# Output sums behind the scores, key scalings in other steps, and a third feed-forward piece of 128 channels in a one-core windowed-attention kernel

## The reference: six layers of windowed attention and feed-forward beside a state-space part

```python
x = L0_attn_x                                  # 16 sequences x 256 tokens x 128
xn = _layernorm(x)
s = state_space_part(xn)                       # about a tenth of the time, at the start
h = xn
for i in range(6):
    h = attn_layer(shift_tokens(h), Wqkv[i], q_scale[i], k_scale[i], Wo[i]) + h
    h = ffn_layer(shift_tokens(h), ln_g[i], ln_b[i], W1[i], b1[i], W2[i], b2[i]) + h
return x + s * silu(h)

def attn_layer(x, Wqkv, qs, ksc, Wo):          # 16 heads of 64, window 32
    q, k, v = split(x @ Wqkv)
    q, k = l2norm(q) * qs, l2norm(k) * ksc
    q = q * cos * scale + rotate_half(q) * sin * scale
    k = k * cos / scale + rotate_half(k) * sin / scale
    attn = softmax(mask(q @ k_window.T * 8.0)) # own and previous window of 32
    return (attn @ v_window) @ Wo

def ffn_layer(x, g, b, W1, b1, W2, b2):        # 341 inner channels
    xn = (x - mean(x)) / sqrt(var(x) + 1e-5) * g + b
    a, gate = split(xn @ W1 + b1)
    return (a * gelu(gate)) @ W2 + b2
```

## Time and profile before

| | us |
|---|---|
| median of 3 runs | 3596.34 |
| the profiled execution | 3596.09 |
| its span | 3594.3 |
| PE busy | 3394.7 (94%) |
| DVE busy | 3151.4 (88%) |
| ACT busy | 2999.4 (83%) |
| POOL busy | 2877.3 (80%) |
| idle of POOL ahead of L1345 | 460.1 |
| idle of POOL ahead of L1359 | 74.0 |
| idle of POOL ahead of L1365 | 64.3 |
| idle of PE ahead of L847 | 59.6 |

### The profile page before, as it was taken

The page is one execution under the profiler, slowest core; times in us unless marked ns, Lnnn a source line. Parts: engine busy times, 40 slices in busy tenths (PEclk is TensorE's granted clock), DMA queues, the critical chain, the costliest instruction groups (busy, mean ns, idle before and its releaser), DMA issues.

```text
span 3594.3 us, 92498 instructions
## 1 busy us (share of the span) xinstructions
PE 3394.7 (94%) x29710; PEld 2110.8 (59%) x29710; DVE 3151.4 (88%) x10872; ACT 2999.4 (83%) x8812; POOL 2877.3 (80%) x2383
## 2 busy tenths in 40 slices
PE   7887999999999999999999999999999999999998
PEld 3444656656666666666656666666666656666665
DVE  7998988988988888988988988988988988988986
ACT  6554888888888888888888888888888888888887
POOL 6887887888887888887888887888887888887883
PEclk9998999999999999999999999999999999999999
DMA  5443322333323333322333322333332333332332
GB/s 164 141 133 124 113 99 102 108 115 108 115 101 101 106 112 106 116 103 99 107 115 107 116 102 99 110 116 103 115 106 96 108 118 105 114 106 99 106 103 92
DMA packets 261726, 396.22 MB, mean 110 GB/s; under 512 B 45566, under 2 KB 86588, under 8 KB 261244
## 3 DMA queue, kind: packets, MB, share of 16 engines
q1 hardware_dynamic: 261244, 390.30, 32.4%
HBM read 157.91 MB, written 6.03 MB: 46 GB/s over the span
## 4 chain that ended last, share of the span: by engine, by line
PE 53%; DVE 17%; POOL 14%; issue 7%; ACT 6%; DMA 2%; SPq 1%; DVEq 0%; POOLq 0%; ACTq 0%
PE bank L886 9%; PE bank L875 7%; PE bank L847 6%; PE bank L360 5%; PE bank L362 5%; PE bank L361 5%; DVE ab L1610 4%; PE bank L914 4%; PE bank L829 4%; POOL rot L1359 4%; POOL pr L1345 4%; PE bank L856 4%; DVE wide L1502 3%; PE bank L857 3%; DVE sm L1655 2%
## 5 line engine op out<-in xcount | busy, mean ns | idle before, releaser
L1184 ACT ACTIVATE pr<-sm,nb,rq 128x128 f32<-128x128 f32 (+1 forms) x3072 | 1518.0, 502 | 10.8 <-DVE nb L1661 10.7
L1345 POOL TENSOR_TENSOR pr<-pr,rden 128x640 f32<-128x640 f32 x768 | 966.2, 1258 | 460.1 <-DVE rden L1635 457.7
L1359 POOL TENSOR_TENSOR rot<-ab,swp 128x512 f32<-128x512 f32 x760 | 978.0, 1287 | 74.0 <-DMA swp<-ab 73.4
L1610 DVE TENSOR_TENSOR ab<-bank,ltab 128x1024 f32<-128x1024 f32 x760 | 925.1, 1217 | 80.6 <-PE bank L362 66.7
L1655 DVE CUSTOM_DVE_ANT_0 sm<-bank,mask 128x128 f32<-128x128 f32 (+1 forms) x3072 | 839.4, 328 | 47.5 <-PE bank L847 42.1
L1184 ACT ACTIVATION_READ_ACCUMULATOR pr<-sm,nb,rq 128x1 f32 x3072 | 599.5, 195 | 0.0
L847 PEld LDWEIGHTS bank<-rot 64*64 64x64 f32 x12288 | 288.1, 132 | 436.0 <-issue 364.7
L1365 POOL TENSOR_TENSOR rot<-rot,rkb 128x512 f32<-128x512 f32 x384 | 492.3, 1289 | 64.3 <-DMA rkb<-k_scratch 64.1
L1642 DVE COPY pt<-bank 128x512 f32<-128x512 f32 x768 | 531.3, 692 | 10.2
L875 PE MATMUL bank<-pt,vtok 128*64 128x160 f32 (+1 forms) x6144 | 461.6, 292 | 29.4 <-ACT vtok L1198 29.4
L1172 ACT ACTIVATE sq<-bank 128x512 f32<-128x512 f32 x768 | 452.6, 589 | 43.2 <-DVE ab L1610 19.9
(11 more groups left out here) (213 smaller groups left out, 5743.7 us busy)
## 6 DMA issues: line engine op xcount, KB each, us to landing
swp<-ab SPq DMA_DIRECT2D x1520, 128.0 KB, 2.0
rkb<-k_scratch SPq DMA_DIRECT2D x768, 128.0 KB, 2.9
rot<-c_scratch SPq DMA_DIRECT2D x64, 256.0 KB, 3.3
sq<-c_scratch SPq DMA_DIRECT2D x64, 256.0 KB, 3.3
xs<-xT SPq DMA_DIRECT2D x95, 128.0 KB, 2.3
xs<-xT SPq DMA_DIRECT2D x95, 127.5 KB, 2.4
raw<-Wqkv SPq DMA_DIRECT2D x48, 128.0 KB, 2.7
wo<-Wo SPq DMA_DIRECT2D x6, 512.0 KB, 4.6
```

Source lines behind the costliest of these rows:

```text
L1184: ins = act.activation(pr[:, s % 4, i, t, 0:P + WINDOW * t], sm[:, s % 2, i, cs], ACT.Exp, bias=nb[:, s, t, i:i + 1], scale=head_scale(rq, ...
L1345: ins = pool.tensor_tensor(pr[:, e % 4, :, :, :], pr[:, e % 4, :, :, :], rden[:, e, :, :].rearrange("p t i -> p i t").unsqueeze(3) .to_bro ...
L1359: pool.tensor_tensor(rot[:, PAIRS * (j % 2) + j // 2, :], ab_of(j, 0, lead), swp_of(j, lead), ALU.add).then_inc(qk_rot, 1)
L1610: dve.tensor_tensor(ab_both(j, lead).rearrange("p i (b t) -> p i b t", b=GB), seqs(qk_bank(j, lead)[:, :]).unsqueeze(1).to_broadcast(shape ...
```

## The change

It has five parts.

1. `outputs` is called directly behind `scores`, ahead of the entries `dn`, `wo`, `rqT`, `cen` and of `down` and `project_out`.
2. `SCALE_STEPS`: pair 1's scaling moves from step 14 of the turn before to step 0, pair 3's from step 2 to step 4.
3. `SPREAD_STEPS`: pair 5's spread moves from step 4 to step 5.
4. `KEYS_FIRST`: at step 13 pair 7's scaling stands ahead of the rotation.
5. `FCH`: the third piece of the feed-forward is channels 213 to 340, 128 wide; its first 43 channels repeat those of the second piece, and their rows of `w2` are zero (one memset).

```diff
-FCH = [(0, 128), (128, 128), (256, FF - 256)]
+FCH = [(0, P), (P, P), (FF - P, P)]
+AGAIN = 3 * P - FF
...
- 4: ('cur', 5)}
+ 5: ('cur', 5)}
 SCALE_STEPS = {13: [('cur', 7)],
+ 0: [('cur', 1)],
  1: [('cur', 2)],
+ 4: [('cur', 3)],
...
- 14: [('next', 0), ('next', 1)],
- 2: [('cur', 3)],
+ 14: [('next', 0)]}
...
+KEYS_FIRST = 13
...
-                sp_e.dma_start(w2[0:FCH[2][1], 2:3, :], W2[bass.ds(layer, 1), 256:FF, :].rearrange("l p c -> p l c"))\
+                sp_e.dma_start(w2[AGAIN:P, 2:3, :], W2[bass.ds(layer, 1), 256:FF, :].rearrange("l p c -> p l c"))\
...
                     if cur is not None:
                         scores(s)
+                    if s % 2 == 0 and s < 6 and prev is not None:
+                        outputs(s, s // 2 + 5, prev)
+                    if s % 2 == 0 and s >= 6 and cur is not None:
+                        outputs(s, s // 2 - 3, cur)
                     bank_work(s, ("dn", "wo", "rqT", "cen"))
...
-                    if s % 2 == 0 and s < 6 and prev is not None:
-                        outputs(s, s // 2 + 5, prev)
-                    if s % 2 == 0 and s >= 6 and cur is not None:
-                        outputs(s, s // 2 - 3, cur)
...
+                    if s == KEYS_FIRST and cur is not None:
+                        scale_k(PAIRS - 1, cur)
                     if s < 2 and cur is not None:
                         rotate(s + 14, cur)
...
                     for role, p in SCALE_STEPS.get(s, ()):
-                        if group_of(role, o) is not None:
+                        if s != KEYS_FIRST and group_of(role, o) is not None:
...
+            dve.memset(w2[0:AGAIN, 2, :], 0.0)
```

More of the change, by code:

```diff
@@ L115 @@
  2: ('cur', 4),
- 4: ('cur', 5)}
+ 5: ('cur', 5)}
 SCALE_STEPS = {13: [('cur', 7)],
+ 0: [('cur', 1)],
  1: [('cur', 2)],
+ 4: [('cur', 3)],
+ 5: [('cur', 4)],
  7: [('cur', 5)],
  9: [('cur', 6)],
- 14: [('next', 0), ('next', 1)],
- 2: [('cur', 3)],
- 5: [('cur', 4)]}
+ 14: [('next', 0)]}
 SCORE_TILES = [(0, 0, 0), (1, 32, 32), (2, P, P - WINDOW), (3, P + 64, P + 32)]
+KEYS_FIRST = 13
 HALVES = np.arange(DH).reshape(2, DH // 2).T.reshape(-1)
```

## The result

The changed kernel takes 3613.52 us (median of 4 runs, 3612.5 to 3614.68); before, beside it, 3596.65. The ratio is 1.0044, 95% interval 1.0032 to 1.0055: some 17 us slower; 3612 was forecast. The same kernel measured again beside the later experiments gave 1.0045 (1.0033 to 1.0058). The profiled execution has a span of 3610.7 us.

What follows compares the result with a forecast made beforehand. It took TensorE's gapless stretch, then a VectorE and ScalarE chain from clamp to products 13, to set the period. Outputs and centring 1, late spread 7.5, scale 7 first 4 + 4: 16.5 us, so 3612 us; range 3578 to 3632.

Steps and rivals of the forecast that it cites:

- What bounds the kernel: Per item: TensorE's gapless stretch, then VectorE and ScalarE from step 9's clamp to products 13; scores 14 wait gains 0.
- Outputs at steps 0, 2, 4: TensorE's gapless stretch: cheaper transitions save 0.15 us at each of three steps, 0.45 us per item, 21 us in all.
- Centring late: Step 8, outputs ahead of centring: ScalarE's centred copy starts 0.92 us later, putting 0.47 us per item on the chain.
- gain and loss together +1 us: Early outputs' -0.45 us and late centring's +0.47 leave +0.02 per item, +1 us over 46 items.
- the two don't add: At step 9's clamp: the spread's 0.2 us lies under ScalarE's 0.47, so a plain item pays nothing more.
- Late spread: Pair 5's spread behind swap 5 and shift: scale 5 2.1 us later; 20 items pay 0.14 to 0.80, 7.5 us.
- the 3.5 us from issue to use: Time from issuing pair 5's spread DMAs to scale 5's use, taken from spread 7 and scale 6.
- Scale 7 first: Step 13: rotate 11 moves back 1.25 us; 4 us from 17 items plus 4 us from a dozen splitting weights.
- Other scales: Scale 1 at step 0 and scale 3 at step 4 fall where GpSimd waits for VectorE's reciprocals anyway: 0.
- wide piece: Third feed-forward piece: six weight loads per item grow from 154 to 189 ns, under matmuls: 0, at most 10 us.
- The sum: 1 + 7.5 + 4 + 4 = 16.5 us on top of 3596.1 us, so 3612 us forecast.
- Rival C: Spread takes 0.6 us more than 3.5, the clamp bounds every item: 22 us, 3634; chance 0.09.

Runs made afterwards that it cites:

- outputs alone: The kernel before with outputs directly behind scores at every even step, so ahead of centring at step 8; nothing else changed: 3591.67 us, ratio 0.9976.
- one number in a table: The kernel before with outputs early at steps 0, 2, 4 and spread of key pair 6 at step 6 instead of 7: 3571.51 us, ratio 0.9926.

## Why the prediction was right, point by point

- *What bounds the kernel.* Right. The chain through clamp, products 13, square, table load and gelu sets the period; removing the GpSimd wait ahead of scores 14 lengthened the gelu wait to 1.23 us and gave nothing.
- *Outputs at steps 0, 2, 4: -21.* Right: -20 alone, 0.44 of 0.45 us in the floor.
- *Centring late: +0.47 per item, +22.* Right in the floor (+0.48), wrong in the total (+14). The step that failed is "gain and loss together +1 us": outputs alone measured -9. I counted what each item loses at the seam, and not that the same lateness hides GpSimd's late DMAs. I had used this very rule one paragraph later ("the two don't add").
- *Late spread: +7.5.* The place and the mechanism were right: scale 5 waits 2.50 us, where 2.1 was forecast, VectorE waits for rotation 6, and the loss beyond ScalarE's 0.47 is at the clamp. The size was off: 18 us within the change, 32 alone. The term that was too small is the 3.5 us from issue to use. They were 3.88 in the plain item, so the clamp there is 0.45 later and not 0.2, level with ScalarE, and an item in which GpSimd is any later goes past it: 14.5 us in 27 items instead of 7.5 in 20. As an estimate from these numbers, 0.4 us more in each of 20 to 27 items is 8 to 11 us. It is not a delay that GpSimd carries on through steps 10 to 13: these are no longer than with the spread put back.
- *Scale 7 first: +8.* About right: +10 alone, 4 to 6 within the change. The wait ahead of scores 14 did turn into a wait for the gelu.
- *Other scales, wide piece: 0.* The piece is right by its own run, and scale 3 by the waits of step 7. Scale 1 at step 0 had no run of its own, only those with others.
- *The sum.* 1 + 7.5 + 8 became -9, +18 and some +5: 3612 and 3613.5 agree because one term was too high and another too low by about as much, and that is luck. Rival C's mechanism (the clamp becomes the bound) is what happened in 27 of the 46 items, more than its 0.09 says, although the DMA was only 0.4 us later than I had it and not 0.6.

## What to carry to other kernels

Two delays that end at the same point don't add, so read the slack of every engine at such a seam before you sum; the same holds for a gain. A delay that just fits under another one leaves no room: 0.4 us more on one DMA doubled this term. To learn where a delay is paid, compare two traces step by step: here 14.5 of 14.9 us lay in one step of 16, although GpSimd had hardly a gap in the five after it. And a DMA that an engine waits for in such a stretch is worth issuing a step earlier even where the wait looks hidden: here one number in a table was worth 7 (by ratios) to 10 us (by medians), with intervals that just overlap.

## What the runs showed of the hardware

A wait of TensorE of 1.62 us ahead of `a`, in a turn in which it had been busy 3.89 of the 5.51 us up to its end, was followed by a stretch at a granted clock of 0.59 that took 1.5 us more. A wait as long, after a stretch as busy, in the 23rd item was not, nor were six more of the ten waits of 1.6 us in that trace, nor any of the 30 in that of scale 7 first. So a delay that reaches TensorE can cost nearly twice its length, but mostly it doesn't. The 35 ns by which six weight loads per item grew cost nothing that could be measured.
